# One pipeline over batches for the last two stages of a two-layer gated cross-attention kernel

## Chip, core and metric

The kernel runs on one core of one Trainium2 chip. The metric is the device time of one execution in microseconds; the kernel before has a median of 1914.06 us over three runs (1909.35 to 1925.1).

## What is computed

Eight batches of 512 tokens of width 512 (fp32), with a context of 77 rows a batch. Four residual blocks follow one another:

```python
x = x + tanh(g_xattn[0]) * L0_xattn(layernorm(x), ctx, ctx, Wq, bq, Wk, bk, Wv, bv, Wo, bo)   # 16 heads
x = x + tanh(g_ffn[0])   * L0_ffn(layernorm(x), router, 8 routed experts (top 2), 2 shared)
# the last two are what the change touches
def L1_xattn(h, v):
    probs = softmax(einsum('bsd,bvd->bsv', h, v), axis=-1)
    return einsum('bsv,bvd->bsd', probs, v)
x = x + tanh(g_xattn[1]) * L1_xattn(layernorm(x), ctx)
def L1_ffn(x):                                  # D = 512, hidden = 2048
    h = act_quant(x) @ weight_quant(w1).T       # 8 bit per token, ternary weights
    h = silu(depthwise_conv3(h) + conv_b)       # three taps along the tokens
    return act_quant(h) @ weight_quant(w2).T
x = x + tanh(g_ffn[1]) * L1_ffn(layernorm(x))
```

## The kernel before

The program runs in four blocks, each with its own instruction stream for every engine and semaphores between them; a block ends with a barrier. `attention` and `experts` come first. They leave, in DRAM, the residual x2 and the results of the experts for each slot (`ys_d`), and the quantised weights `w1q_d` and `w2q_d`. A "row tile" is 128 tokens; a batch has four (TB = 4).

`fuse` (from L1360) is a software pipeline over batches. In step s it combines batch s + 1 (`combine_first`, `combine_second`, L1606 and L1613 on VectorE: x2 + gate1 * y1 + gate2 * y2, with y1 and y2 gathered by eight indirect DMAs from Pool, L1517), takes its statistics (`bn_stats`, L1589) and normalises it on ScalarE (L1580). In the same step batch s is transposed (L1684), scored against the context (L1691), exponentiated (L1568), transposed again (L1695, copied to `prT` in L1571) and multiplied with the context (L1701), and VectorE adds the residual (L1661) and takes statistics (L1666). Batch s - 1 is normalised (L1563), its row maxima are taken (L1633), it is rounded on ScalarE (L1576, copies that add and later subtract a large constant) and dequantised on VectorE (L1601). The residual x3 and the quantised xd are written to DRAM scratch (L1494, L1499). The inverse roots (`rstd`, L1523 and L1525) are on Pool.

`ffn` (from L1706) is a second pipeline over batches with f_ps as a ring of three PSUM banks (RING = 3) and three hidden buffers `h` (HB = 3). In round s TensorE first multiplies two of the four row tiles of batch s - 2 with w2 (`down(0)`, `down(1)`, 17 matmuls each, L1963 and L1965), transposes the maxima of batch s - 1 (`max_transposes`, L1998), and then runs the 16 up tiles of batch s (`up(m)`, eight matmuls each, L1988), with the row of scales (L2004) behind up 1 and the other two down tiles behind up 5 and up 11. At the end it transposes batch s + 1 (L2033), whose high and low parts ScalarE (L1871) and VectorE (`low`, L1917) write. For each up tile ScalarE writes the middle tap (L1854), VectorE adds the other two (`taps`, L1890 and L1893), and ScalarE applies silu (L1836). VectorE takes the absolute maxima over eight tiles at a time (`half_max`, L1901). The tiles of batch s - 1 are multiplied with the row of scales on Pool (L1826) and rounded by a ScalarE copy (`lift_tile`, L1841), in the places that `lifts` names. VectorE adds the result to x3 (`outputs`, L1883).

Every engine executes its instructions in the order written, so an instruction that waits holds up all behind it on its engine.

## Time and profile before

| | |
|---|---|
| median of three runs | 1914.06 us |
| the profiled execution | 1918.68 us, of which the span is 1917.2 us |
| TensorE busy in the span | 1653.6 us (86%), weight loads 1304.5 us |
| VectorE, ScalarE, Pool busy | 1137.7, 794.9 and 588.0 us |
| mean granted clock of TensorE | 0.904 of full speed |

Times of rows are microseconds from the start of the span. PE is TensorE (PEld its weight loads), DVE VectorE, ACT ScalarE, POOL Pool (GpSimd), SP the queue of SyncE; a q behind an engine's name is a DMA that its queue issues. Granted clock 1.0 is 2.4 GHz and 0.5 is 1.2 GHz. The busy time of matmuls overlaps from one to the next, so the pace of a run of matmuls is read from the timeline and not from the mean of one.

### The profile page before, as it was taken

To read this page: it belongs to the slowest core of one execution; us is meant where nothing else is said; L and a number is where in the kernel's file an instruction comes from. 1 tells how busy PE (TensorE), PEld (TensorE's weight loads), DVE (VectorE), ACT (ScalarE), POOL (GpSimd) and SP (SyncE) were. 2 spreads that over 40 slices of the span, in tenths; PEclk is the share of its full clock that TensorE was granted. 3 is DMA by queue.
4 is the path that set the end of the run, shared out by engine and by line. 5 is a ranking of instruction groups with operands and counts; after the bars stand their busy time and mean duration, and the time that the engine had idled before them with its cause. 6 is when DMAs were issued, how large, how long until landed. Compare 5 with 4: busy or idle time off the path is not lost. (4 is left out here: it accounts for less than half of the span.)

```text
span 1917.2 us, 26044 instructions
## 1 busy us (share of the span) xinstructions
PE 1653.6 (86%) x8636; PEld 1304.5 (68%) x8636; DVE 1137.7 (59%) x1946; ACT 794.9 (41%) x1417; POOL 588.0 (31%) x541
## 2 busy tenths in 40 slices
PE   7599999999866999998999999837674889999997
PEld 5578888788745888886778888624343666666664
DVE  3587878878745344532223333258875777777775
ACT  2243433434313422222334443325563556566653
POOL 0133323333212444464331000065513243344440
PEclk9798989889967999999999999957666899999999
DMA  3112122121129889984443333287743111111102
GB/s 124 44 45 88 55 77 88 44 88 55 67 74 351 286 304 316 321 282 138 162 139 107 107 108 106 94 303 287 256 148 110 44 44 66 66 66 38 51 23 88
DMA packets 108196, 252.02 MB, mean 131 GB/s; under 512 B 15027, under 2 KB 15027, under 8 KB 103912
## 3 DMA queue, kind: packets, MB, share of 16 engines
q1 hardware_dynamic: 65272, 121.98, 19.0%
q0 software_dynamic: 17056, 67.12, 9.7%
q10 hardware_dynamic: 25808, 62.14, 9.2%
q8 instruction: 35, 0.57, 0.1%
q14 instruction: 25, 0.20, 0.0%
HBM read 147.13 MB, written 101.97 MB: 130 GB/s over the span
## 5 line engine op out<-in xcount | busy, mean ns | idle before, releaser
L1275 PE MATMUL e_u_ps<-e_w,e_xeT 128*128 128x512 f32 x1596 | 393.1, 398 | 10.8 <-DVE e_xeT L1180 10.8
L1275 PEld LDWEIGHTS e_u_ps<-e_w,e_xeT 128*128 128x128 f32 x1596 | 293.1, 189 | 73.3 <-DVE e_w L1229 8.9
L1988 PE MATMUL b_f_ps<-b_xdT,w1q 128*128 128x512 f32 x1024 | 254.1, 404 | 11.5 <-DVE b_h L1893 9.4
L1988 PEld LDWEIGHTS b_f_ps<-b_xdT,w1q 128*128 128x128 f32 x1024 | 191.4, 190 | 64.8 <-DVE b_h L1893 18.3
L1826 POOL TENSOR_TENSOR b_h<-b_h,b_srow 128x512 f32<-128x512 f32 x112 | 143.6, 1342 | 245.9 <-ACT b_srow L1847 245.9
L1286 PE MATMUL e_y_ps<-e_w,e_hT 128*128 128x512 f32 x798 | 209.9, 405 | 4.3 <-DVE e_hT L1211 2.8
L1286 PEld LDWEIGHTS e_y_ps<-e_w,e_hT 128*128 128x128 f32 x798 | 143.3, 190 | 31.0 <-issue 4.0
L1854 ACT ACTIVATE b_h<-b_f_ps,cb,cw 128x512 f32<-128x512 f32 x128 | 104.2, 814 | 124.5 <-PE b_f_ps L1988 124.3
L1890 DVE SCALAR_TENSOR_TENSOR b_h<-b_f_ps,cw,b_h 128x511 f32<-128x511 f32 x128 | 95.9, 749 | 85.9 <-ACT b_h L1854 85.7
L490 ACT ACTIVATE pT<-t_ps 77x512 f32<-77x512 f32 x128 | 71.9, 590 | 119.0 <-PE t_ps L691 119.0
L465 POOL TENSOR_TENSOR prob<-prob,ri 128x1232 f32<-128x1232 f32 x32 | 74.9, 2341 | 115.3 <-DVE ri L572 115.3
L1211 DVE TENSOR_TENSOR e_hT<-e_h_ps,e_hT 128x256 fp32r<-128x256 f32 x69 | 29.3, 424 | 134.8 <-ACT e_hT L1046 134.8
L1965 PE MATMUL b_o_ps<-w2q,b_h 128*128 128x512 bf16 x448 | 106.2, 392 | 0.0
L730 PE MATMUL m_ps<-wo,oT 128*128 128x512 f32 x384 | 96.3, 407 | 7.1 <-DVE oT L598 7.0
L744 PE MATMUL m_ps<-xT,wq 128*128 128x256 f32 x768 | 98.3, 289 | 1.4 <-DVE xT L554 1.4
L1836 ACT ACTIVATE b_h<-b_h 128x512 f32<-128x512 f32 x128 | 86.7, 677 | 30.8 <-DVE b_h L1893 30.8
L1893 DVE SCALAR_TENSOR_TENSOR b_h<-b_f_ps,cw,b_h 128x511 f32<-128x511 f32 x128 | 96.2, 752 | 4.5
L691 PE MATMUL t_ps<-ident,prob 128*77 128x128 f32 x512 | 90.8, 340 | 7.6 <-ACT pT L490 4.9
L744 PEld LDWEIGHTS m_ps<-xT,wq 128*128 128x128 f32 x768 | 95.4, 196 | 1.8 <-DVE xT L554 1.8
L442 POOL TENSOR_TENSOR ve<-mv,eps 128x2 f32<-128x2 f32 x32 | 6.2, 194 | 289.6 <-DVE mv L583 289.6
L730 PEld LDWEIGHTS m_ps<-wo,oT 128*128 128x128 f32 x384 | 73.0, 194 | 27.9 <-DVE oT L598 11.5
L985 POOL DMA_INDIRECT slots_in_scratch<-e_srow,e_scol x64 | 71.8, 1122 | 56.7 <-DMA e_srow<-xn_scratch 37.3
(221 smaller groups left out, 2869.1 us busy)
## 6 DMA issues: line engine op xcount, KB each, us to landing
e_xe<-slots_in_scratch SPq DMA_DIRECT2D x69, 256.0 KB, 2.6
experts_out_scratch<-e_ye ACTq DMA_DIRECT2D x69, 256.0 KB, 2.0
xin<-in_x SPq DMA_DIRECT2D x16, 512.0 KB, 3.8
xres<-in_x SPq DMA_DIRECT2D x16, 512.0 KB, 4.5
x_scratch<-x SPq DMA_DIRECT2D x32, 256.0 KB, 2.1
xn_scratch<-xn SPq DMA_DIRECT2D x32, 256.0 KB, 2.1
e_xe<-xn_scratch SPq DMA_DIRECT2D x32, 256.0 KB, 4.2
e_fraw<-in_w1T ACTq DMA_DIRECT2D x8, 1024.0 KB, 8.3
```

The source lines that it names most:

```text
L691: mm = pe.transpose(t_ps[0:C, t[("p", j, g)] % 2, i * P:(i + 1) * P], prob[:, j, g * HG + i, :], ident[:])
L730: mm = pe.matmul(m_ps[:, m[f"w{j}"] % 2], oT[:, pa, k, j * P:(j + 1) * P], wo[:, pb, k, :], start=(k == 0 and (pa, pb) == PASSES[0]), stop ...
L744: mm = pe.matmul(m_ps[:, m[f"q{i}"] % 2, g * W2:(g + 1) * W2], wq[:, pa, k, mt * P:(mt + 1) * P], xT[:, pb, k, :], start=(k == 0 and (pa, ...
L1275: mm = pe.matmul(u_ps[:, i], xeT[:, pa, k], w[:, par, pb, k * 2 * HID:(k + 1) * 2 * HID], start=(k == 0 and (pa, pb) == PASSES[0]), stop=( ...
L1286: mm = pe.matmul(y_ps[:], hT[:, pa, i * KH + k], w[:, par, pb, W1N + k * D:W1N + (k + 1) * D], start=(i == 0 and k == 0 and (pa, pb) == PA ...
L1826: pool.tensor_tensor(ht, ht, srow[:], ALU.mult).then_inc(u_done, 1)
L1836: act.activation(ht, ht, ACT.Silu).then_inc(h_done, 1)
L1854: act.activation(tile(s, m), f_ps[:, (s * KF + m) % RING], ACT.Identity, bias=cb[:, m:m + 1], scale=cw[:, m, 1:2]).then_inc(mid_tap, 1)
L1890: dve.scalar_tensor_tensor(out=ht[:, 1:S], in0=f[:, 0:S - 1], scalar=cw[:, m, 0:1], in1=ht[:, 1:S], op0=ALU.mult, op1=ALU.add).then_inc(pr ...
L1893: dve.scalar_tensor_tensor(out=ht[:, 0:S - 1], in0=f[:, 1:S], scalar=cw[:, m, 2:3], in1=ht[:, 0:S - 1], op0=ALU.mult, op1=ALU.add).then_in ...
L1965: mm = pe.matmul(o_ps[:, j % 2], rounded(s - 2, k, j), w2q[:, k, :], start=False, stop=(k == KF - 1))
L1988: mm = pe.matmul(f_ps[:, u % RING], w1q[:, k, m * P:(m + 1) * P], xdT[:, part, k], start=(k == 0 and part == 0), stop=(k == KD - 1 and par ...
```

## The change

`fuse` and `ffn` are replaced by one block, `tail`. A round s (from -2 to 9) holds what is still to be done for five batches:

- `down`: the four down tiles of batch s - 2 and its output (D0 to D3 below). All four stand ahead of the up tiles of the round now. The two `attend` banks and the down tiles share the two banks of o_ps.
- `quant`: maxima, scales, products and lifts of batch s - 1. Ten of the 16 products on Pool stand ahead of the combining, six behind it.
- `up`: the 16 up tiles of batch s with their taps and silus. The ring has four banks (RING = 4), which the transposes of the fusing part use too. There are two hidden buffers (HB = 2) in place of three.
- `cross`: the whole fusing part of batch s + 1, spread over the instruction streams between the up tiles. The quantised batch is not sent to DRAM any more but transposed in the same round.
- `comb_next`: the combining of batch s + 2. ScalarE multiplies y1 and y2 with their gates (`gate_experts`), Pool makes the two additions into the residual X, which stays on chip until the output (four buffers, XB = 4), and Pool issues the gathers two row tiles ahead, right behind the additions that free a buffer.

The dequantisation and the small steps of the inverse root move from VectorE to Pool. The order in which each engine takes the parts of a round is written out in the `run` of each engine.

```diff
         experts(nc, n)
-
-        n.w1q = keep("w1q", [P, KD, DH], FR)
-        n.w2q = keep("w2q", [P, KF, D], BF16)
-        n.cw = keep("cw", [P, KF, 3], F32)
-        n.cb = keep("cb", [P, KF], F32)
-        n.g2 = keep("g2", [P, 1], F32)
-        fuse(nc, n)
-        ffn(nc, n)
+        tail(nc, n)
...
+    RING = 4
+    HB = 2
+    XB = 4
...
+        X = sb("x", [P, XB, TB, D])
+        y = sb("y", [P, 4, D])
...
+            for s in range(-2, B + 2):
+                run(s, 0 <= s - 2, 0 <= s - 1 < B, 0 <= s < B, 0 <= s + 1 < B, s + 2 < B)
...
+        lifts = {0: (3,), 1: (4,), 2: (5,), 3: (6,), 4: (7,), 5: (8,), 6: (9,), 12: (10,), 13: (11,), 14: (12,), 15: (13, 14, 15)}
...
         @block.sync
+            def run(s, down, quant, up, cross, comb_next):
+                if down:
+                    sp.wait_ge(y_done, (s - 1) * TB)
+                    sp.dma_start(n.tile_rows(n.out, (s - 2) * TB, TB), X[:, (s - 2) % XB]).then_inc(out_done, 16)
+                if comb_next:
+                    if s + 2 >= XB:
+                        sp.wait_ge(out_done, (s - 1) * 16)
+                    load(s + 2)
...
         @block.gpsimd
+            def combine(b, j):
+
+                t = b * TB + j
+                xb = X[:, b % XB, j]
+                pool.wait_ge(gated, t + 1)
+                pool.wait_ge(x2_in[b % XB], 16 * (b // XB + 1))
+                pool.tensor_tensor(xb, xb, y[:, 2 * (j % 2)], ALU.add).then_inc(comb_first, 1)
+                pool.wait_ge(comb_first, t + 1)
+                pool.tensor_tensor(xb, xb, y[:, 2 * (j % 2) + 1], ALU.add).then_inc(comb, 1)
+                if t + 2 < B * TB:
+                    hold(pool, comb, t + 1, n.passed_pool)
+                    gather((t + 2) // TB, (t + 2) % TB)
...
+                if s == 0:
+                    column_sums()
+                if quant and up:
+                    pool.wait_ge(row_done, s)
+                    products(0, 10)
+                if comb_next:
+                    combine(s + 2, 0)
+                    combine(s + 2, 1)
+                if cross:
+                    rstd(1, mv2_done, s + 1, nmr2_done)
+                if comb_next:
+                    combine(s + 2, 2)
+                    combine(s + 2, 3)
+                if cross:
+                    for j in range(TB):
+                        pool.wait_ge(q_done, (s + 1) * TB + j + 1)
+                        pool.tensor_scalar(xw[:, j], xw[:, j], MAGIC, dq[:, j:j + 1], ALU.subtract,
+                                           ALU.mult).then_inc(xd_done, 1)
+                if quant and up:
+                    products(10, KF)
+                if comb_next:
+                    rstd(0, mv1_done, s + 2, nmr1_done)
...
         @block.scalar
+                def gate_experts(j):
+                    t = (s + 2) * TB + j
+                    act.wait_ge(y_in[j % 2], 32 * (t // 2 + 1))
+                    for i in range(2):
+                        yb = y[:, 2 * (j % 2) + i]
+                        ins = act.activation(yb, yb, ACT.Copy, scale=gate[:, i, t:t + 1])
+                    ins.then_inc(gated, 1)
+
+                b = s + 1
+                if cross:
+                    act.wait_ge(nmr1_done, b + 1)
+                    if b >= 1:
+                        act.wait_ge(xdt_full, b * TB)
+                    for j in range(TB):
+                        act.activation(xw[:, j], X[:, b % XB, j], ACT.Identity, bias=nmr[:, 0, j:j + 1],
+                                       scale=rs[:, 0, j:j + 1]).then_inc(xn_done, 1)
+                    for j in range(TB):
+                        act.wait_ge(xt_full, b * TB + j + 1)
+                        act.activation(xT[:, j], f_tiles("x", b, j), ACT.Copy).then_inc(xt_copied, 1)
+                if quant:
+                    scale_row()
+                    if up:
+                        for m in range(3):
+                            lift_tile(m)
+                if cross:
+                    act.wait_ge(nm_done, b + 1)
+                    for j in range(TB):
+                        act.activation(pr[:, j], q_ps[:, 1, j, 0:C], ACT.Exp, bias=nm[:, j:j + 1],
+                                       accum_out=su[:, j:j + 1]).then_inc(e_done, 1)
+                if up and s >= 2:
+                    act.wait_ge(y_full, (s - 1) * TB)
+                if up and s == 0:
+                    act.wait_ge(cw_done, 2)
+                if up and s == 1:
+                    act.wait_ge(wsum_steps, 4)
+                for m in range(KF):
+                    if up:
                         act.wait_ge(f_full, s * KF + m + 1)
+                        act.activation(tile(s, m), f_bank("f", s, m), ACT.Identity, bias=cb[:, m:m + 1],
                                        scale=cw[:, m, 1:2]).then_inc(mid_tap, 1)
                         if m >= 1:
                             silu(m - 1)
+                    if cross and m == 1:
+                        act.wait_ge(p_full, b + 1)
+                        act.activation(prT[:], q_ps[0:C, 0], ACT.Copy).then_inc(p_copied, 1)
+                    if quant and up:
+                        for r in lifts.get(m, ()):
+                            lift_tile(r)
+                    if comb_next and m in (2, 3, 5, 6):
+                        gate_experts(m - 2 if m < 4 else m - 3)
+                    if cross and m == 7:
+                        act.wait_ge(nmr2_done, b + 1)
+                        for j in range(TB):
+                            act.activation(xw[:, j], X[:, b % XB, j], ACT.Identity, bias=nmr[:, 1, j:j + 1],
+                                           scale=rs[:, 1, j:j + 1]).then_inc(x4_done, 1)
+                    if cross and m == 10:
+                        act.wait_ge(sc_done, b + 1)
+                        for j in range(TB):
+                            act.activation(xw[:, j], xw[:, j], ACT.Copy, bias=MAGIC,
+                                           scale=sc[:, j:j + 1]).then_inc(q_done, 1)
+                if up:
                     silu(KF - 1)
                 elif quant:
                     for m in range(KF):
                         lift_tile(m)
+                if cross:
                     for j in range(TB):
+                        act.wait_ge(xdt_full, b * TB + j + 1)
+                        act.activation(xdT[:, 0, :, j], f_tiles("d", b, j), ACT.Copy).then_inc(xdt_hi, 1)
...
         @block.vector
+                if down:
                     outputs(0)
                     outputs(1)
                 if quant:
                     token_scales()
+                if down and (up or not quant):
+                    outputs(2)
+                    outputs(3)
+                if cross:
+                    dve.wait_ge(s_full, b + 1)
+                    dve.tensor_reduce(nm[:], q_ps[:, 1, :, 0:C], AX.X, ALU.max, negate=True).then_inc(nm_done, 1)
+                for m in range(KF):
+                    if up:
                         taps(m)
+                    if cross and m == 0:
+                        dve.wait_ge(e_done, b * TB + TB)
+                        dve.reciprocal(ri[:], su[:]).then_inc(ri_done, 1)
+                        dve.wait_ge(ri_done, b + 1)
+                        dve.tensor_scalar(rt[:], ri[:], tg[:, 1:2], None, ALU.mult).then_inc(rt_done, 1)
+                        dve.wait_ge(rt_done, b + 1)
+                    if cross and m in (2, 4):
+                        fused(m - 2)
+                        fused(m - 1)
+                    if cross and m == 4:
+                        aggregate(1, stats[0] - TB, mv2_done)
+                    if cross and m in (7, 8):
+                        row_max(2 * m - 14)
+                        row_max(2 * m - 13)
+                    if cross and m == 8:
+                        row_scales()
+                    if up and m == 10:
+                        half_max(0)
+                if quant and not up:
                     dve.wait_ge(row_done, s)
                     for m in range(KF):
                         ht = tile(s - 1, m)
                         dve.tensor_tensor(ht, ht, srow[:], ALU.mult).then_inc(u_done, 1)
                         if m in (3, 7):
                             outputs(2 + m // 4)
+                if comb_next:
+                    for j in range(TB):
+                        dve.wait_ge(comb, (s + 2) * TB + j + 1)
+                        dve.bn_stats(st[:, 0, j], X[:, (s + 2) % XB, j]).then_inc(st_done, 1)
+                    stats[0] += TB
+                    aggregate(0, stats[0] - TB, mv1_done)
+                if cross:
                     low(0)
+                if up:
                     half_max(1)
+                if cross:
                     for j in range(1, TB):
                         low(j)
...
         @block.tensor
+                if s == B + 1:
                     down_all()
                     return
+                if down:
+                    down_tile(0)
+                    down_tile(1)
+                if cross:
+                    normed_transposes()
                 if quant:
                     max_transposes()
+                if down:
+                    down_tile(2)
+                if quant:
                     scale_row()
+                if down:
+                    down_tile(3)
+                if cross:
+                    scores()
+                for m in range(KF):
+                    if up:
+                        up_tile(m)
+                    if cross and m == 0:
+                        prob_transposes()
+                    if cross and m in (1, 3):
+                        attend(m - 1)
+                        attend(m)
+                if cross:
+                    quantised_transposes()
```

In `normed_transposes` row tile j waits for its bank, last read by `low(j)` of the batch before; `attend(2)` and `attend(3)` wait for `fused(0)` and `fused(1)`; `down_tile(2)` waits for `outputs(0)`.

## Rows read from the trace of the kernel before

**Rows 1.** Stretches: length, then each engine's busy us, granted clock, DMA share, GB/s.

```profile
1315.42:1337.19 21.77, 14.75 (x62) 9.20 (x61) 18.65 (x46) 12.54 (x26) 10.74 (x14) 0.69 0.72 251
...
1671.00:1724.40 53.40, 49.88 (x222) 34.53 (x221) 38.65 (x46) 32.85 (x53) 20.53 (x16) 0.97 0.17 60
```

**Rows 2.** Timeline, stage boundaries: start, us, engine, line, instruction, idle before it.

```profile
1242.02 0.34 ACTq L1058 DMA_DIRECT2D experts_out_scratch<-e_ye  x1
...
1270.72 2.93 ACT L1580 ACTIVATE f_xn<-f_x,nmr,f_rs 128x512 f32<-128x512 f32 x4 [28.86 <-DVE nmr L1649]
...
1457.80 0.20 POOL L1812 MEMSET b_lift<- 128x128 bf16 x1 [12.38 <-POOLq L1364]
...
1469.80 10.54 PE L1988 MATMUL b_f_ps<-b_xdT,w1q 128*128 128x512 f32 x44 [1.41 <-DVE b_xdT L1917]
...
1895.24 0.53 PEld L1972 LDWEIGHTS b_f_ps<-b_wsum,b_lift 128*128 128x128 bf16 x3
```

**Rows 3.** Timeline of TensorE: down, up, scores, attended tiles, maxima transposes.

```profile
1608.12 3.62 PE L1965 MATMUL b_o_ps<-w2q,b_h 128*128 128x512 bf16 x16
...
1716.40 4.46 PE L1965 MATMUL b_o_ps<-w2q,b_h 128*128 128x512 bf16 x16
...
1620.66 7.71 PE L1988 MATMUL b_f_ps<-b_xdT,w1q 128*128 128x512 f32 x32
...
1315.42 3.69 PE L1691 MATMUL f_s_ps<-f_ctraw,f_xT 128*128 128x77 f32 x32
...
1371.53 7.20 PE L1701 MATMUL f_o_ps<-f_craw,prT 77*128 77x512 f32 x8 [0.68 <-ACT prT L1571]
...
1615.25 1.04 PE L1998 MATMUL b_q_ps<-ident,b_am 128*128 128x128 f32 x8
```

**Rows 4.** Groups by line, VectorE, both stages: count, busy us, mean ns, idle before.

```profile
L1893 DVE SCALAR_TENSOR_TENSOR b_h<-b_f_ps,cw,b_h 128x511 f32<-128x511 f32 x128 | 96.2, 752 | 4.5
...
L1901 DVE TENSOR_REDUCE b_am<-b_h 128x512 f32<-128x4096 f32 x16 | 70.6, 4410 | 0.7 <-ACT b_h L1836 0.7
...
L1666 DVE BATCH_NORM_STATS2 f_st<-x 128x6 f32<-128x512 f32 x32 | 22.0, 686 | 0.1
```

**Rows 5.** Timeline of ScalarE: tap, silu, two lifts, four normalisations.

```profile
1854.12 0.81 ACT L1854 ACTIVATE b_h<-b_f_ps,cb,cw 128x512 f32<-128x512 f32 x1
...
1854.82 0.66 ACT L1836 ACTIVATE b_h<-b_h 128x512 f32<-128x512 f32 x1
...
1855.39 1.22 ACT L1841 ACTIVATE b_h<-b_h 128x512 f32<-128x512 f32 x2
...
1307.20 2.92 ACT L1580 ACTIVATE f_xn<-f_x,nmr,f_rs 128x512 f32<-128x512 f32 x4
```

**Rows 6.** Timeline of ScalarE around the first silu of the stage.

```profile
1473.84 0.81 ACT L1854 ACTIVATE b_h<-b_f_ps,cb,cw 128x512 f32<-128x512 f32 x1 [1.06 <-PE b_f_ps L1988]
...
1474.67 1.28 ACT L1836 ACT_TABLE_LOAD   x1
...
1475.96 0.67 ACT L1836 ACTIVATE b_h<-b_h 128x512 f32<-128x512 f32 x1
```

**Rows 7.** Pool: groups by line (as rows 4), and from issue to landing of L1517.

```profile
L1826 POOL TENSOR_TENSOR b_h<-b_h,b_srow 128x512 f32<-128x512 f32 x112 | 143.6, 1342 | 245.9 <-ACT b_srow L1847 245.9
...
L1525 POOL TENSOR_TENSOR f_rs<-f_ve,f_half 128x4 f32<-128x4 f32 x16 | 16.4, 1026 | 1.3
...
L1546 POOL TENSOR_SCALAR cw<-cwr,mean 128x48 f32<-128x48 f32 x1 | 0.4, 437 | 0.0
...
L1517 POOL DMA_INDIRECT y<-experts_out_scratch,ycol x64 | 64.0, 999 | 23.7 <-issue 16.7 <-POOL ycol L1513 6.7 <-DVE f_mv L1595 0.3
...
DMA to landing us min/median/max: 3.4/6.3/8.9
```

**Rows 8.** DMA issues of the fusing stage: count, KB each, us to landing.

```profile
f_x<-x_scratch SPq DMA_DIRECT2D x8, 1024.0 KB, 10.5
...
cwr<-in_conv_w SPq DMA_DIRECT2D x1, 24.0 KB, 12.1
```

715 lines of the change are left out of this document (257 added, 458 removed).

## The prediction

> **What bounds the kernel now.** I read the table of stretches first, then the boundaries of the stages in order of time, then the rows of one round of each stage. Up to 1242 us attention and experts run; the diff leaves them alone. The fusing stage reaches from there to 1457.8, the feed-forward stage to the end at 1917.2 [rows 2]: 215.8 + 459.4 = 675.2 us that the change rewrites. A fusing round takes 21.8 us, of which VectorE is busy 18.7 and TensorE 14.8 at a granted clock of 0.69. A feed-forward round takes 53.4 us; TensorE is busy 49.9 of them at 0.97, VectorE 38.7, ScalarE 32.9, Pool 20.5 [rows 1]. The up tiles run at 1.93 (32 matmuls in 7.7) and a down tile takes 3.7 with the one matmul ahead of it [rows 3]. So the first is bound by VectorE, the second by TensorE, and one batch costs 75.2 us in both. The remaining 675.2 - 8 x 75.2 = 74 us are beginnings and ends.
>
> **What the merged round costs each engine.** The arithmetic work of a batch stays; what goes is the x3/xd round trip (hidden, but for the 12 us from 1457.8 to the first up tile at 1469.8 [rows 2]).
> - TensorE: 49.9, plus 16 transposes (about 2.2, twice the eight of 1.04), scores 3.7, four transposes of probabilities (0.6) and four attended tiles. Their eight instructions took 7.2 at the low clock (1.2 GHz), so 3.6 at 2.4. Sum 60 [rows 1, 3].
> - ScalarE: 32.9 + two normalisations of 2.9 + four rounding copies 2.5 + xT copies 2.4 + exps 1.3 (four of 77 columns, estimated at half a full copy each) + prT 0.6 + eight gatings 5 (a 128x512 ACTIVATE issues every 0.6 to 0.7) + two table loads 2.6 = 53 [rows 1, 5, 6]. Exp and Silu need different tables and now alternate; before, each was loaded once in these stages.
> - VectorE: 38.7 + fused additions and both statistics (4 x 0.75 + 8 x 0.69) + row maxima (2.7, at 0.69) + small ones 2 = 52 [rows 1, 4]. The combining additions and the dequantisation leave it.
> - Pool: 20.5 + eight additions at 1.3 (row: 1.34) + eight gathers at 1.3 + four dequantisations 5 + two rstd (one power at 1.03 and three small steps each, 4) = 50 [rows 1, 7]. The dequantisation (128x512 TENSOR_SCALAR) has no row on Pool; between 0.44 (the 48-column one) and 2.1 (its slope from 0.2 extended) I take 1.3, like the two-input row. It lies between the q copies and the last six products, whose lifts ScalarE reaches later: 0 us at 1.3, 2 us at 2.1 (the next down tile waits for the last lift).
>
> **Where the round's time comes from.** No engine is full at 60, so order decides. I walk one full round; 0 is the end of TensorE's last quantised transpose. All costs are from [rows 3 to 7].
> - Front (TensorE). D0, D1 (3.67 each) end at 7.3. VectorE meanwhile does four statistics, low 0, half_max 1 (4.4), low 1 to 3, and is through at 9.1. The transposes of normalised rows need low j's PSUM bank, so they end at 9.8. Maxima 10.8, D2 14.5, scale row 15.5, D3 19.2, scores 22.9. No down tile overlaps the up tiles any more: with HB = 2 ScalarE may not write tile 0 before D3 is read out, where before two down tiles lay between up tiles. The row with the first down tile of a round at 4.46 instead of 3.62 [rows 3] shows 0.8 us for a clock that fell in the sparse tail of the round; I put the front at 23.3.
> - Head of the up tiles. Up 0 and the transposed probabilities (after max and exps) and up 1 end at 27.8. prT, without which attend 0 can't start, stands on ScalarE behind middle tap 1 (0.8), the Silu table (1.3) and silu 0 (0.6): copied at 31.1. TensorE waits 3.3 us there with up 2 behind attend 0 and 1. Up 2 ends 34.9, its tap 35.7, gate 0 ends 38.0.
> - Gather chain. Pool can't combine row tile 0 before 38.0. Two additions 2.7, 0.8 from a held wait to a gather (6.7 us over eight batches, in the row of the gathers), the second gather at 42.8 (1.0 + 0.3 later), tile 1 the same: its second gather starts at 48.5. A gather lands 3.4 to 8.9 us after issue, median 6.3 in a stage whose DMA share was 0.72. Here that share is about 0.2, so I take 4 (near the minimum): landed 52.5. ScalarE reaches gate 3 at about 50.5 and waits 2; gate 3 ends 53.7. All middle taps queue behind it.
> - Residual. Batch s+2's load waits on the SP queue for the store of batch s-2, which starts when D3 is read out (20). At 10.5 us for either 1 MB transfer [rows 8] it is in by 41, and Pool wants it at 38: 3 us at most. That row is from the stage with a DMA share of 0.72, so I take 0.
> - Tail. Tap 7, silu 6, four normalisations: 57.9. Tap 8, its VectorE taps 60.2, row maxima and scales 62.1, taps 9 63.6, silu 9, q copies 66.7. VectorE: taps 10, half_max 0 to 69.4, taps 11 70.9. Then four tiles with one lift each (0.70 + 0.57 + 0.62 = 1.9 on ScalarE): last middle tap 76.5, taps 78.0, last quantised transpose and last lift 78.7.
> Round: 79 us, 55.7 of them from up 0 to the last transpose, against 75.2 before. The merged engines' idle time is in-order waiting.
>
> **The table loads, by row and by page.** The row shows the load beginning 0.02 us after the ACTIVATE before it and Silu beginning 0.01 after it [rows 6]: 1.28 us in all. The Trainium skill (ScalarE: Activation LUTs, What ACT_TABLE_LOAD costs) adds a drain of about 1380 ns to every switch. By that the load on prT's path would cost 1.4 us more, some 10 us over seven rounds, and the forecast would be about 1952. The rows show no such gap, so the sum goes without it.
>
> **Sum.**
> - Start, 1242.4 to up 0 of batch 0: Pool waits for the constants before its first addition. They landed 12.1 us after issue behind two 1 MB loads and the gathers, at about 1260 [rows 8]; one 1 MB load less is ahead of them now, so I take 1257.8 (bounds 1252 to 1262). Four combining steps alternate with gathers (two of them issued only after tile 0 and 1): Pool is through at about 1280.7, rstd 1.9, normalisation at 1282.7, where before it was at 1270.7 [rows 2]. Scores, exps and attended tiles at the low clock, fused 1304; two more gather landings before x4, dequantised 1327, batch 1's transposes and scores before up 0: 1337.5. So 95 us (bounds 87 to 103).
> - Round 0, no lifts and no down tiles: 54 + front of round 1 (no D) 18 = 72.
> - Rounds 1 to 5: 5 x 79 = 395.
> - Round 6, without gates: 51 + front of round 7 (no scores) 17 = 68.
> - Round 7 (TensorE's 16 up tiles, 33.5), D0, D1, maxima, D2, scale row, D3 17, then from the last batch's down tiles to the end as before, 1895.2 to 1917.2 = 22 [rows 2]: 72.5.
> Together 702.5 against 675.2: +27.3. On the profiled span 1917.2 this is a span of 1944.5; with the 1.5 us around it, 1946. The median of the runs lies 4.6 below the profiled run's 1918.7, so I forecast 1942 us, 1.5% slower.
>
> **Rivals.**
> - *Latencies are absorbed and the round becomes engine-bound (faster).* If the prT copy and gate 3 find their inputs ready (a gather landing within 2 us, no waiting at attend 0), the up part falls from 55.7 to what VectorE needs: 16 x 1.45 + 6 + 3.2 + 4.4 + 2 = 39, plus 3 before its first tap and 3 for the last: 45. Six rounds of 11 less: 1876 us. For it: ScalarE, VectorE and Pool all have over 25 us idle per round in my walk, so there is idle time to recover. Against: prT stands in one queue behind a table load and a tap whose input comes after it. It decides below 74.8 us a round (4.2 less). Chance 0.22.
> - *No measurable change.* The start is 8 shorter and each round 2 to 3 shorter (a gate nearly in time, up tiles' taps closer together): 1916 us. Chance 0.17.
> - *The low clock settles in (slower still).* From up 11 on TensorE works less than half the time, as in the fusing round, whose granted clock was 0.69 [rows 1]. If D0 to D2 run at the low level (7.3 each instead of 3.7, the first two half hidden), the front grows by 5: six rounds, +30: 1972 us. Against: 0.97 in the feed-forward rounds, which have the same sparse transposes. Chance 0.14.
> - *A gather lands in 6.3 as before:* +2.3 a round, 1958; within the forecast's own range.
> Forecast 0.47, own range 1925 to 1965 (start +-8, landing 3.4 to 6.3, dequantisation 0 to 2 and residual 0 to 3 us a round).
>
> About 1% is what a measurement of this kernel can tell from no change. Faster by over 1% (below 1895): the first rival and a little of the second, 0.24. Within 1%: the second and the low end of the forecast, 0.20. Slower: 0.56. The range 1885 to 1975 leaves out most of the first rival, 0.16, and a few hundredths above.
>
> **What would show it.** Right: about 79 us between the maxima transposes of successive rounds; TensorE waiting 3 us at attend 0 for prT; ScalarE waiting for y (gather) before gate 3 and Pool for gate 0; 15 or so table loads of 1.28; up 0 of batch 0 near 1337; an end near 1944. Wrong: TensorE over 85% busy in a round; no wait at the gates; a round below 75; rows of the gated tiles or Pool's dequantisation far from 0.6 and 1.3; D tiles at 7 us.

## The result and the profile after

The changed kernel takes **2008.5 us** (median of four runs, 2001.4 to 2010.0), the kernel before 1914.1 in the runs beside it (median of three; a fourth took 4084.6 us and is left out). The ratio of the means is **1.047 (1.041 to 1.054)**, slower by 4.7%. The forecast was slower by 1.5% (1942 us), its range ended at 1975.

The page of the changed kernel, its span and the busy times of the engines:

```profile
span 2007.7 us, 25829 instructions
...
PE 1673.9 (83%) x8636; PEld 1319.0 (66%) x8636; DVE 1081.7 (54%) x1826; ACT 850.1 (42%) x1493; POOL 737.0 (37%) x660
```

The table of stretches (the columns of [rows 1]): one full round, then within it up tile 1 with the wait behind it, the 10 us that follow, and a stretch near the round's end.

```profile
1587.20:1672.50 85.30, 68.33 (x289) 46.60 (x288) 51.44 (x78) 52.87 (x88) 49.82 (x44) 0.86 0.17 54
...
1601.30:1606.70 5.40, 2.08 (x11) 1.40 (x9) 3.55 (x6) 4.26 (x7) 3.83 (x4) 0.96 0.73 253
1606.70:1616.70 10.00, 8.70 (x20) 5.32 (x20) 2.16 (x3) 3.58 (x7) 0.00 (x0) 0.68 0.00 0
...
1646.70:1665.00 18.30, 11.91 (x44) 7.05 (x43) 14.11 (x21) 11.84 (x21) 14.19 (x13) 0.70 0.00 0
```

One merged round takes 85.3 us where the two rounds of [rows 1] took 75.2. ScalarE, VectorE and Pool are busy 53, 51 and 50 us of it, as the sums in the prediction had it (53, 52, 50). TensorE is busy 68, not 60: the granted clock is 0.86 over the round and 0.68 in the 10 us behind the wait of 1603 to 1607.

The timeline at the boundaries that answer [rows 2]: last store of the experts, the constants' wait, the first up tile of batch 0, a first down tile:

```profile
1244.27 0.34 ACTq L1047 DMA_DIRECT2D experts_out_scratch<-e_ye  x1
...
1267.80 0.41 POOL L1628 TENSOR_SCALAR t_cw<-t_cwr,mean 128x48 f32<-128x48 f32 x1 [14.90 <-DMA t_cb<-in_conv_b]
...
1349.99 2.09 PE L1898 MATMUL t_f_ps<-t_xdT,t_w1q 128*128 128x512 f32 x8
...
1575.59 5.31 PE L1876 MATMUL t_o_ps<-t_w2q,t_h 128*128 128x512 bf16 x16
```

TensorE at the head of the up tiles (up 1; attended tiles 0 and 1; up 2 and 3):

```profile
1601.30 2.08 PE L1898 MATMUL t_f_ps<-t_xdT,t_w1q 128*128 128x512 f32 x8
1606.73 3.78 PE L1948 MATMUL t_o_ps<-t_craw,t_prT 77*128 77x512 f32 x4 [3.35 <-ACT t_prT L1695]
1609.52 5.91 PE L1898 MATMUL t_f_ps<-t_xdT,t_w1q 128*128 128x512 f32 x16
```

ScalarE in the same round: table load, silu 0, the copy of the probabilities; middle tap 2; gate 3; lift 10:

```profile
1604.24 1.28 ACT L1638 ACT_TABLE_LOAD   x1
1605.54 0.66 ACT L1638 ACTIVATE t_h<-t_h 128x512 f32<-128x512 f32 x1
1606.09 0.58 ACT L1695 ACTIVATE t_prT<-t_q_ps 77x512 f32<-77x512 f32 x1
...
1613.65 0.80 ACT L1689 ACTIVATE t_h<-t_f_ps,t_cb,t_cw 128x512 f32<-128x512 f32 x1 [6.42 <-PE t_f_ps L1898]
...
1631.31 1.34 ACT L1656 ACTIVATE t_y<-t_y,gate 128x512 f32<-128x512 f32 x2 [1.94 <-DMA t_y<-experts_out_scratch,slot]
...
1652.92 0.67 ACT L1643 ACTIVATE t_h<-t_h 128x512 f32<-128x512 f32 x1 [2.78 <-POOL t_h L1596]
```

Pool in the same round, the first addition, the dequantisations and the six late products:

```profile
1616.85 1.28 POOL L1561 TENSOR_TENSOR t_x<-t_x,t_y 128x512 f32<-128x512 f32 x1 [11.72 <-ACT t_y L1656]
...
1643.65 7.98 POOL L1614 TENSOR_SCALAR t_xw<-t_xw,t_dq 128x512 f32<-128x512 f32 x4 [1.76 <-ACT t_xw L1709]
1651.61 7.59 POOL L1596 TENSOR_TENSOR t_h<-t_h,t_srow 128x512 f32<-128x512 f32 x6
```

The groups by line (count, busy us, mean ns, idle before) of the operations that the sum priced: products, dequantisation, gates.

```profile
L1596 POOL TENSOR_TENSOR t_h<-t_h,t_srow 128x512 f32<-128x512 f32 x112 | 142.1, 1306 | 96.7 <-ACT t_srow L1649 96.7
...
L1614 POOL TENSOR_SCALAR t_xw<-t_xw,t_dq 128x512 f32<-128x512 f32 x32 | 63.8, 2000 | 28.0 <-ACT t_xw L1709 28.0
...
L1656 ACT ACTIVATE t_y<-t_y,gate 128x512 f32<-128x512 f32 x56 | 37.1, 712 | 27.3 <-DMA t_y<-experts_out_scratch,slot 27.3
```

The walk of a round, predicted and measured (us from the start of the round's first down tile, here 1575.2; the last transpose of the round before ended 0.2 us later):

| mark | predicted | after |
|---|---|---|
| up 0 starts | 23.3 | 23.6 |
| up 1 ends | 27.8 | 28.2 |
| probabilities copied | 31.1 | 31.5 |
| middle tap 2 starts | 34.9 | **38.5** |
| gate 0 ends | 38.0 | 41.6 |
| gate 3 ends | 53.7 | 57.5 |
| four normalisations end | 57.9 | 61.5 |
| q copies end | 66.7 | 70.2 |
| taps 11 end | 70.9 | 74.2 |
| round ends | 78.7 | **85.5** |

Two places carry nearly the whole difference of a round: 3.2 us between the copied probabilities and middle tap 2, and 3.5 us behind taps 11. Ahead of them and between them the walk holds within 0.4 us.

### The profile page after: what moved, and what is told of

It is laid out like the page before. It is cut to its first block and busy times, and to the rows that moved or that the text cites. A ratio compares the mean times of both kernels' runs of the same rounds, so it can differ in the third digit from the quotient of the medians.

```text
span 2007.7 us, 25829 instructions
## 1 busy us (share of the span) xinstructions
PE 1673.9 (83%) x8636; PEld 1319.0 (66%) x8636; DVE 1081.7 (54%) x1826; ACT 850.1 (42%) x1493; POOL 737.0 (37%) x660
## 3 DMA queue, kind: packets, MB, share of 16 engines
q1 hardware_dynamic: 48520, 90.53, 13.5%
## 5 line engine op out<-in xcount | busy, mean ns | idle before, releaser
L1898 PE MATMUL t_f_ps<-t_xdT,t_w1q 128*128 128x512 f32 x1024 | 278.1, 429 | 52.0 <-DVE t_h L1763 52.0
L1898 PEld LDWEIGHTS t_f_ps<-t_xdT,t_w1q 128*128 128x128 f32 x1024 | 204.5, 204 | 118.5 <-DVE t_h L1763 65.7
L1760 DVE SCALAR_TENSOR_TENSOR t_h<-t_f_ps,t_cw,t_h 128x511 f32<-128x511 f32 x128 | 95.4, 745 | 152.8 <-ACT t_h L1689 152.6
L1596 POOL TENSOR_TENSOR t_h<-t_h,t_srow 128x512 f32<-128x512 f32 x112 | 142.1, 1306 | 96.7 <-ACT t_srow L1649 96.7
L1689 ACT ACTIVATE t_h<-t_f_ps,t_cb,t_cw 128x512 f32<-128x512 f32 x128 | 103.3, 807 | 70.9 <-PE t_f_ps L1898 70.3
L479 ACT ACTIVATE pT<-t_ps 77x512 f32<-77x512 f32 x128 | 72.2, 591 | 120.6 <-PE t_ps L680 120.6
L1876 PE MATMUL t_o_ps<-t_w2q,t_h 128*128 128x512 bf16 x448 | 113.3, 411 | 0.0
L1638 ACT ACTIVATE t_h<-t_h 128x512 f32<-128x512 f32 x128 | 86.0, 672 | 43.1 <-DVE t_h L1763 42.8
L1643 ACT ACTIVATE t_h<-t_h 128x512 f32<-128x512 f32 x128 | 83.8, 678 | 36.4 <-POOL t_h L1596 34.5
L1763 DVE SCALAR_TENSOR_TENSOR t_h<-t_f_ps,t_cw,t_h 128x511 f32<-128x511 f32 x128 | 96.2, 752 | 4.5
```

Of the source, the lines that this page charges most:

```text
L1596: pool.tensor_tensor(ht, ht, srow[:], ALU.mult).then_inc(u_done, 1)
L1638: act.activation(ht, ht, ACT.Silu).then_inc(h_done, 1)
L1689: act.activation(tile(s, m), f_bank("f", s, m), ACT.Identity, bias=cb[:, m:m + 1], scale=cw[:, m, 1:2]).then_inc(mid_tap, 1)
L1760: dve.scalar_tensor_tensor(out=ht[:, 1:S], in0=f[:, 0:S - 1], scalar=cw[:, m, 0:1], in1=ht[:, 1:S], op0=ALU.mult, op1=ALU.add).then_inc(pr ...
L1763: dve.scalar_tensor_tensor(out=ht[:, 0:S - 1], in0=f[:, 1:S], scalar=cw[:, m, 2:3], in1=ht[:, 0:S - 1], op0=ALU.mult, op1=ALU.add).then_in ...
L1876: mm = pe.matmul(acc, rounded(s - 2, k, j), w2q[:, k, :], start=False, stop=(k == KF - 1))
```

## The experiments

Each kernel was timed on the same chip as the kernel before. The ratio to it stands first; the changed kernel's is 1.047. A round is the distance of two successive reductions of the transposed maxima on VectorE (L1745). Rounds 1 to 5 are the steady ones: in the changed kernel the first of them takes 83.1 us and the other four 85.2 to 85.3. The stages ahead, which are the same in every one of these kernels, ended anywhere between 1228 and 1245 us in the profiled executions, so the length of a round says more than the total of one execution. Diffs are extracts; "..." stands for lines left out.

**1. The copy of the probabilities ahead of middle tap 1.**

```diff
-                    if cross and m == 1:
+                    if cross and m == 0:
                         act.wait_ge(p_full, b + 1)
                         act.activation(prT[:], q_ps[0:C, 0], ACT.Copy).then_inc(p_copied, 1)
```

> Starts from the changed kernel (2008.5 us). ScalarE copies the transposed probabilities (prT) behind middle tap 0 instead of behind middle tap 1 and silu 0. Nothing is left out. Theory A (the wait of TensorE for this copy, 3.35 us a round, also drops TensorE's clock to its low level for the next tiles, which costs as much again): the wait goes, granted clock in the stretch behind it stays near 1.0, a round falls by 6 to 7 us (85.2 to about 79), 7 rounds give about 45 us: 1964. Theory B (only the wait counts, the tiles behind it are slow for another reason): 3.3 us a round, about 23 us: 1985. Theory C (the gathers and gates behind it set the round, the wait is covered): under 1 us a round, 2002 to 2008.

Ratio 1.021 (1.017 to 1.025), median 1958.9; a round takes 78.3. TensorE in its timeline (up 1, attended 0 and 1, up 2 and 3):

```profile
1558.30 2.09 PE L1898 MATMUL t_f_ps<-t_xdT,t_w1q 128*128 128x512 f32 x8
1560.22 1.88 PE L1948 MATMUL t_o_ps<-t_craw,t_prT 77*128 77x512 f32 x4
1561.54 4.21 PE L1898 MATMUL t_f_ps<-t_xdT,t_w1q 128*128 128x512 f32 x16
```

The wait is gone, the attended tiles take 1.88 instead of 3.78, the two up tiles 4.21 instead of 5.91. A round is 6.9 us shorter, twice the wait: theory A.

**2. TensorE kept busy through the wait.**

```diff
+                    if up and cross and m == 1:
+                        empty(f_uses, f_at, ("f", s, 2))
+                        for k in range(14):
+                            pe.matmul(f_bank("f", s, 2), w1q[:, k % KD, 0:P], xdT[:, 0, k % KD], start=True, stop=True)
                     if cross and m in (1, 3):
```

> Starts from the changed kernel. Its order and its waits are kept, but TensorE computes 14 matmuls of 128x512 whose result nobody reads into the free bank of up tile 2, between up tile 1 and the wait for the copied probabilities, about 3.3 us of work in the place of 3.35 us of waiting. Theory A (idling drops the clock): the attended tiles start within 0.5 us of where they did, but they and up tiles 2 and 3 take 1.8 and 1.93 us instead of 2.8 and 3, a round falls by about 3 us, total 1985 to 1990. Theory B (those tiles are slow for another reason, such as their operands or Pool's and VectorE's traffic): no change of the round, 2005 to 2012.

Ratio 1.033 (1.029 to 1.038), median 1982.4; a round takes 81.7. Its timeline (the matmuls that nobody reads, attended tiles, up 2 and 3):

```profile
1582.15 3.33 PE L1984 MATMUL t_f_ps<-t_xdT,t_w1q 128*128 128x512 f32 x14
1585.67 1.98 PE L1948 MATMUL t_o_ps<-t_craw,t_prT 77*128 77x512 f32 x4 [0.19 <-ACT t_prT L1695]
1587.09 4.21 PE L1898 MATMUL t_f_ps<-t_xdT,t_w1q 128*128 128x512 f32 x16
```

The attended tiles start no earlier relative to up 1 (3.4 us behind its end in either), and yet a round is 3.5 us shorter: theory A. Of the 6.9 us, half is the wait and half the low clock that follows it. This separates the two, which experiment 1 could not.

**3. Dequantisation back on VectorE**, behind taps 12 to 15, one tile each.

```diff
-                if cross:
-                    for j in range(TB):
-                        pool.wait_ge(q_done, (s + 1) * TB + j + 1)
-                        pool.tensor_scalar(xw[:, j], xw[:, j], MAGIC, dq[:, j:j + 1], ALU.subtract,
-                                           ALU.mult).then_inc(xd_done, 1)
...
+                    if cross and m >= 12:
+                        j = m - 12
+                        dve.wait_ge(q_done, b * TB + j + 1)
+                        dve.tensor_scalar(xw[:, j], xw[:, j], MAGIC, dq[:, j:j + 1], ALU.subtract,
+                                          ALU.mult).then_inc(xd_done, 1)
```

> Starts from the changed kernel. Only the four dequantisations of a batch go back from Pool to VectorE, one behind each of the taps 12 to 15. Nothing is left out. Theory A (Pool's 4 x 2.0 us delay products 10 to 15, ScalarE waits 2.8 us for product 10 ahead of middle tap 13, and that is on the path): lift 10's wait goes, a round falls by 2 to 3 us (85.2 to about 82.5), in all about 20 us with 8 us of it at the start where the batch 0 dequantisation is on the path too: 1985 to 1990. Theory B (the last stretch is bound by VectorE's taps, which now carry 2 us more): a round stays at 85 or rises by 1, total 2000 to 2012.

Ratio 1.033 (1.027 to 1.039), median 1986.6; rounds 2 to 4 take 81.7 us, round 5 85.2, at a lower granted clock (0.88 over that round; 0.90 to 0.92 in rounds 2 to 4). Lift 10 runs right behind the silu ahead of it (first fence, ScalarE's timeline), and the operation costs VectorE 0.48 us (second, groups by line):

```profile
1637.15 0.69 ACT L1633 ACTIVATE t_h<-t_h 128x512 f32<-128x512 f32 x1 [2.07 <-DVE t_h L1758]
1637.73 0.68 ACT L1638 ACTIVATE t_h<-t_h 128x512 f32<-128x512 f32 x1
```

```profile
L1833 DVE TENSOR_SCALAR t_xw<-t_xw,t_dq 128x512 f32<-128x512 f32 x32 | 15.4, 481 | 1.1 <-ACT t_xw L1704 0.8
```

Theory A, and with 3.5 us a round more than its 2 to 3. The same instruction takes 2.00 us on Pool and 0.48 on VectorE. Batch 0's alone, with nothing beside it, shortens the way from its score maxima to batch 1's from 47.7 to 42.0 us.

**4. The exponentials replaced by a copy with bias**, so that no table is switched. This kernel leaves out the softmax.

```diff
-                        act.activation(pr[:, j], q_ps[:, 1, j, 0:C], ACT.Exp, bias=nm[:, j:j + 1],
+                        act.activation(pr[:, j], q_ps[:, 1, j, 0:C], ACT.Identity, bias=nm[:, j:j + 1],
```

> Starts from the changed kernel. The four exponentials of a batch are replaced by a copy with bias, which needs no table of its own, so that the softmax is not computed and ScalarE's 14 table switches are gone but for one. Theory A (by the rows, the switch back ahead of silu 0 costs 1.28 us on the path to the copied probabilities, the other is hidden in a wait): TensorE's wait falls from 3.35 to about 2.1 us; if the clock still falls behind it, a round falls by 1.3 us, in all about 9 us: 1999. Theory A2 (the same, but the shorter wait keeps the clock up): 1.3 + 3.5 us a round, 1975. Theory B (a switch also drains the engine, about 1.4 us more that the rows don't show): 2.7 us a round, 1990, and the wait falls to 0.7 us.

Ratio 1.033 (1.029 to 1.037), median 1985.3; a round takes 82.0. TensorE (attended tiles, up 2 and 3):

```profile
1596.59 3.01 PE L1948 MATMUL t_o_ps<-t_craw,t_prT 77*128 77x512 f32 x4 [1.92 <-ACT t_prT L1695]
1598.61 5.27 PE L1898 MATMUL t_f_ps<-t_xdT,t_w1q 128*128 128x512 f32 x16
```

TensorE's wait for the copy is 1.92 us instead of 3.35, the same in all seven rounds that have a silu ahead of the copy: 1.43 us less. Of these, 1.28 is the load; without it, silu 0 also starts 0.1 us before middle tap 1 ends (1595.42 and 1595.52), an overlap that is lost where the load lies between them. Under theory B it would have been 2.7. The round fell by 3.2, more than the wait, and that number alone would not have told A2 from B. The attended tiles and up tiles 2 and 3 took 3.01 and 5.27 us, between the values of the changed kernel and of experiment 1, so they ran at the low clock for a shorter time. The outcome lies between A and A2; the exact split of the 3.2 us was not measured.

**5. Gates of tiles 0 and 1 ahead of the exponentials.**

```diff
+                if comb_next and up:
+                    gate_experts(0)
+                    gate_experts(1)
                 if cross:
                     act.wait_ge(nm_done, b + 1)
-                    if comb_next and m in (2, 3, 5, 6):
+                    if comb_next and m in ((5, 6) if up else (2, 3, 5, 6)):
```

> Starts from the changed kernel. ScalarE gates the expert rows of tiles 0 and 1 behind lifts 0 to 2, ahead of the exponentials (their gathers landed a round before), instead of behind middle taps 2 and 3; nothing is left out. The additions on Pool, and so the next gathers, can start some 10 us earlier. Theory A (gather, gate, additions and the fused normalisation behind them lie on the path): gate 3's wait for its gather (1.9 us) goes and four gates (2.3 us) leave the stretch before the normalised rows, a round falls by 3 to 4 us (85.2 to about 81.5), in all 1980 to 1987. Theory B (middle tap 2 and the tiles behind it set the pace because of the low clock): under 1 us a round, 2002 to 2010. The exponentials may start 0.7 us later in either.

Ratio 1.035 (1.031 to 1.039), median 1989.5; rounds 2 to 5 take 82.3 to 84.3. That is 2.4 us a round against the 3 to 4 of theory A: gates do lie on the path, but here they hold the exponentials up (they start 1.30 us behind the maxima of the scores instead of 0.04), and with them the probabilities.

**6. The constants' wait moved behind the first combining.**

```diff
+                if s == -1:
+                    pool.wait_ge(cw_in, 32)
...
-            pool.wait_ge(cw_in, 32)
             whole(run)
```

The two small instructions behind the wait (`cw`, `g2`) move with it.

> Starts from the changed kernel. Pool's wait for the convolution's constants, with the two small instructions behind it, moves from ahead of the first combining (15 us of waiting at the head of its queue) to behind the combining of batch 0. Nothing is left out. Theory A (that wait delays the first combining and so the whole pipeline's start): the first up tile of batch 0 comes 8 to 10 us earlier, total 1998 to 2001. Theory B (the load of the first x tiles lands no earlier than the constants do, being on the same queue ahead of them or sharing its bandwidth): start moves by under 2 us, total 2006 to 2010.

Ratio 1.046 (1.041 to 1.050), median 2009.7. The first combining comes 10 us earlier (1258.6), batch 0's score maxima only 2 us (60.1 us behind VectorE's last instruction of the experts instead of 62.3), and the next stretches give that back. Theory B. The transfers of the changed kernel from 1244 to 1300 us suggest why, and experiment 7 tests it: the busy share of the DMA engines in 40 slices, then issues with KB and us to landing.

```profile
DMA  2237999999999999997999994760016401650000
...
t_w1q<-w1q_scratch POOLq DMA_DIRECT2D x1, 4096.0 KB, 19.3
t_x<-x_scratch SPq DMA_DIRECT2D x3, 1024.0 KB, 18.5
t_w2q<-w2q_scratch SPq DMA_DIRECT2D x1, 2048.0 KB, 21.6
...
t_cb<-in_conv_b SPq DMA_DIRECT2D x1, 8.0 KB, 18.4
```

For some 30 us the DMA engines are 70% busy or more, in most slices over 90%. Of the 13.5 MB moved in this window, 6 are weights that nobody needs before 1340.

**7. The weights loaded later:** experiment 6, with the up weights' load behind the combining of tiles 0 and 1 and the down weights' load behind batch 0's attention. Both loads are taken out where they stood.

```diff
                     combine(s + 2, 1)
+                if s == -2:
+                    pool.dma_start(w1q[:].rearrange("p k f -> p (k f)"), n.w1q_d[:, :]).then_inc(w1_in, 16)
...
+                if s == 0:
+                    sp.dma_start(w2q[:].rearrange("p k f -> p (k f)"), n.w2q_d[:, :]).then_inc(w2_in, 16)
```

> Starts from the changed kernel. Only the start is rearranged: the constants' wait of Pool behind the combining of batch 0, the 4 MB load of the up weights behind the combining of tiles 0 and 1, the 2 MB load of the down weights behind batch 0's attention. Nothing is left out. Theory A (the start is bound by the bandwidth of the transfers, which are 97 to 99% busy for 28 us, and the gathers wait behind the weights): the first combining and the gathers behind it land 4 us after issue instead of 8, batch 0's maxima of the scores come 10 to 15 us sooner, total 1995 to 2000. Theory B (the weights are needed as early as they are loaded, so the first up tile waits for them instead): under 3 us, 2005 to 2012.

Ratio 1.038 (1.033 to 1.042), median 1989.1. Batch 0's score maxima come 50.0 us behind VectorE's last instruction of the experts instead of 62.3, and the rest takes 705 us in both: theory A, 12 us, of which 2 are experiment 6's and 10 the traffic's. The median is 19 us lower; the other 7 are probably no gain of the edit, since the stages ahead ended 7 us earlier in this profile. Its transfers, same view:

```profile
t_w1q<-w1q_scratch POOLq DMA_DIRECT2D x1, 4096.0 KB, 13.0
t_x<-x_scratch SPq DMA_DIRECT2D x3, 1024.0 KB, 10.3
```

**8. Experiments 1, 3 and 5 together.**

> Starts from the changed kernel and makes three edits at once: the probabilities copied behind middle tap 0, dequantisation back on VectorE behind taps 12 to 15, gates of tiles 0 and 1 ahead of the exponentials. Nothing is left out. Theory A (the costs lie one behind another on the same path and add): a round falls by 6.9 + 3.5 + 3 us, 85.2 to 72, total about 1915, beside the kernel before within 1%. Theory B (they cover one another, ScalarE or VectorE sets the middle of the round once the clock is up): a round at 75 to 77, total 1935 to 1950, still slower than before.

Ratio 1.009 (1.006 to 1.011), median 1935.3. Four of the five steady rounds take 74.3 to 76.0, the fifth 81.1. The single gains add to 12.8, the three together give about 10 in the four: between the theories, nearer B. Its stretch of taps 7 to 14 (columns as above) shows what comes next:

```profile
1598.10:1618.10 20.00, 14.23 (x49) 10.15 (x48) 18.12 (x27) 15.63 (x25) 14.14 (x12) 0.83 0.19 52
```

VectorE is busy 18.1 of 20 us there.

**9. Four edits:** the three, with gates 0 and 1 in ScalarE's wait ahead of the scale row, and the start of experiment 7.

```diff
+                if comb_next and up:
+                    gate_experts(0)
+                    gate_experts(1)
                 if quant:
                     scale_row()
```

> Starts from the changed kernel and joins four edits: probabilities copied behind middle tap 0, dequantisation on VectorE behind taps 12 to 15, gates of tiles 0 and 1 in ScalarE's 4.7 us wait ahead of the scale row (not ahead of the exponentials, where they held them up by 1.3 us in the run of three edits), and the later loads at the start. Nothing is left out. Theory A (the edits add, since the start and the rounds follow one another): the three edits gave 1935; the start gives 12 us (first maxima of scores 50 us behind the last expert tile instead of 62), the exponentials 1.3 us in each of 6 rounds: about 1915, within 1% of before (1919). Theory B (in the rounds VectorE is the bound by now, so the earlier exponentials give nothing): 1923. A round is 74 under A, 75.3 under B.

Ratio 1.002 (1.000 to 1.004), median 1925.2, with four steady rounds of 72.2 to 75.1 and one of 78.2: nearer theory B. The start's 12 us arrived. The exponentials again start 0.04 us behind the maxima, but a round gained less than their 1.3 us (74.3 on average in the four, against 75.0 in the four of experiment 8).

**10. VectorE's maximum over tiles 0 to 7 cut in two**, tiles 0 to 3 behind tap 5, tiles 4 to 7 behind tap 10.

```diff
-                    if up and m == 10:
-                        half_max(0)
+                    if up and m == 5:
+                        quarter_max(0)
+                    if up and m == 10:
+                        quarter_max(1)
```

`quarter_max` is `half_max` over four tiles; one VectorE maximum, ahead of `half_max(1)`, joins the two parts.

> As the kernel of four edits, and VectorE's maximum over tiles 0 to 7, 4.4 us at tap 10, is cut in two: tiles 0 to 3 behind tap 5, where VectorE waits for ScalarE, tiles 4 to 7 behind tap 10, and the two joined at the end of the round behind the tiles' last low part. Nothing is left out. Theory A (taps 7 to 15 are bound by VectorE, 18.1 of 20 us busy there): 2.2 us of it leave that stretch, a round falls by 1.5 to 2 us, 10 us in all below the kernel of four edits. Theory B (the wait behind tap 5 is no slack, since what follows it waits for the same chain): no difference, within 3 us.

Ratio 0.999 (0.997 to 1.001), median 1919.0: 6 us less than experiment 9 on the same chip, where A expected 10 and B at most 3. The five steady rounds take 74.1 on average instead of 75.0. In its timeline the next wait stands out, TensorE at attended tile 2 and ScalarE at middle tap 4:

```profile
1641.21 1.10 PE L1969 MATMUL t_o_ps<-t_craw,t_prT 77*128 77x512 f32 x2 [1.41 <-DVE t_x L1790]
...
1646.99 0.80 ACT L1692 ACTIVATE t_h<-t_f_ps,t_cb,t_cw 128x512 f32<-128x512 f32 x1 [5.23 <-PE t_f_ps L1919]
```

**11. Attended tiles 2 and 3 behind up tile 4**, added to experiment 10.

```diff
-                    if cross and m in (1, 3):
-                        attend(m - 1)
-                        attend(m)
+                    if cross and m in (1, 4):
+                        attend(m // 2)
+                        attend(m // 2 + 1)
```

> As the kernel with the maximum cut in two, and TensorE computes the attended tiles 2 and 3 behind up tile 4 instead of ahead of it. Nothing is left out. There they wait for VectorE to free the two banks (1.4 and 0.3 us), and with them up tile 4, for which ScalarE then sat idle 5.2 us; the granted clock in those 10 us is 0.83. Theory A (that wait, and the low clock in it, are on the path): up tile 4 comes 3 to 4 us sooner, a round falls from 74.5 to 71 or 72, 15 to 20 us in all, about 1900: faster than before by 1%. Theory B (the fused rows, the normalisation behind them and VectorE's later taps are the path; up tile 4 early gives only an earlier wait): within 4 us of the kernel it starts from, 1915 to 1923.

Ratio **0.990 (0.986 to 0.993)**, median 1904.1; five steady rounds of 71.4 on average, 2.7 less. Theory A: the in-order queue of TensorE had kept up tile 4, which was ready, behind an attended tile that waited for its bank. ScalarE no longer waits ahead of middle tap 4. How much of the 2.7 us is the wait and how much the clock behind it was not separated. Behind the sparse end of a round the first down tile still runs at the low clock (TensorE: last quantised transposes, first down tile):

```profile
1598.41 1.11 PE L1976 MATMUL t_f_ps<-ident,t_xw 128*128 128x128 f32 x4 [0.94 <-DVE t_xw L1851]
...
1599.75 5.56 PE L1897 MATMUL t_o_ps<-t_w2q,t_h 128*128 128x512 bf16 x16
```

**12. Matmuls that nobody reads in those pauses**, added to experiment 11.

```diff
+                        empty(f_uses, f_at, ("d", b, j))
+                        for k in range(4 if up and j > 0 else 0):
+                            pe.matmul(f_bank("d", b, j), w1q[:, k, 0:P], w1q[:, k, 0:4 * P], start=True, stop=True)
                         pe.wait_ge(xd_done, b * TB + j + 1)
-                        empty(f_uses, f_at, ("d", b, j))
```

> As the kernel with the later attended tiles, and TensorE computes four matmuls of 128x512 that nobody reads ahead of each of the quantised transposes of tiles 1 to 3, where it waits 1.4, 1.2 and 0.7 us for VectorE. Theory A (the pauses of the last 10 us of a round let the clock fall, so that the first down tile behind them takes 5.4 us instead of 3.6): that tile takes 3.6 us, a round falls by 1.8 us, 10 us in all. Theory B (the down tile is covered, the path runs through VectorE's maximum behind it, or the filling delays the transposes as much as it saves): within 4 us of the kernel it starts from.

Ratio **0.988 (0.984 to 0.992)**, median 1899.0; the same five rounds take 70.5. The same stretch in experiment 11 and in this one, where it is one round; then the filling matmuls and the first down tile:

```profile
1526.00:1596.10 70.10, 63.48 (x286) 44.26 (x284) 52.55 (x83) 51.60 (x87) 41.87 (x40) 0.91 0.21 65
...
1526.00:1596.10 70.10, 62.47 (x302) 44.20 (x301) 53.93 (x85) 53.13 (x89) 41.95 (x40) 1.00 0.22 65
...
1655.04 1.22 PE L1975 MATMUL t_f_ps<-t_w1q 128*128 128x512 f32 x4 [0.21 <-DVE t_h L1766]
...
1656.74 3.62 PE L1897 MATMUL t_o_ps<-t_w2q,t_h 128*128 128x512 bf16 x16
```

The clock is 1.00 over this round (0.93 to 1.00 in the five, 0.90 to 0.93 in experiment 11) and the first down tile takes 3.62 instead of 5.56. In the steady rounds this gave 0.9 us each on average, half of theory A's 1.8; where the other half went was not traced; the totals of 11 and 12 (1904 and 1899) differ by less than their runs spread, so in the total the gain is likely, not shown.

## Why the prediction was right in direction and short in size

**Right: the waits and the engine sums.** No engine is the bound, the waits of the in-order queues are. TensorE waits 3.35 us at attended tile 0 (said: 3.3), gate 3 waits 1.94 us for its gather (said: 2), which landed 3.8 us after issue (said: 4), Pool waits 11.7 us for gate 0, the front takes 23.6 (said: 23.3). A gate instruction takes 0.71 us as it lies between others. The residual's load cost nothing. The rivals with a faster or an equal time needed those waits to be absorbed, and none was.

**Wrong step 1, the clock behind the wait.** The walk priced the wait of 3.3 us for the copied probabilities and then ran attended tiles and up 2 at the high level (2.4 GHz). The row of the slow down tile, 4.46 instead of 3.62 [rows 3], had been read as 0.8 us for the sparse tail only, and the rival on the low clock looked at the down tiles alone. It compared the tail with the fusing round as one where TensorE "works less than half the time", but the row of that round has it busy 14.75 of 21.77 us [rows 1]. Behind the wait TensorE ran at a mean of 0.68 for 10 us, and middle tap 2 came 3.6 us later than walked. Experiments 1 and 2 show it: 6.9 us for wait and clock, 3.5 for the clock alone. Over rounds 1 to 5 that is 17 of the missing 31 us.

**Wrong step 2, the price of the dequantisation on Pool, and what queues behind it.** The bounds were 0.44 and 2.1 us; I took 1.3, like the two-input row, with 0 us on the path. It takes 2.00, near the upper bound as written, whose price of 2 us a round stood in the text; the row shows lift 10 waiting 2.8 us, and experiment 3 gives 3.5 for the whole. My 2 us assumed that only the last lift is late. But lift 10 stands ahead of middle tap 13 in ScalarE's queue, so the taps behind it are late with it. The upper bound was also worked out wrong: 0.2 us and the slope of the 48-column row (0.24 us for 48 columns) give 2.7 us for 512 (an estimate), not 2.1. So neither row had the price; the measured 2.00 lies halfway between 1.3 and 2.7. The fault is that a middle value with 0 us on the path was taken where the row left a range of 0.44 to 2.7. Five rounds: 14 to 17 us.

**Wrong step 3, the start.** Said 95 us from the last expert store to up 0, measured 105.4. The constants landed at 1267.8, not 1257.8, since I priced them with the row of the fusing stage [rows 8] and one load less ahead. The last of them, the 8 KB of the convolution's bias, took 18.4 us to land, as the rows of experiment 6 show; 6 MB of weights that this program loads in the same stretch were not in the sum. Even so the wait named in the sum was not the cost: without it (experiment 6) 2 us come back, without it and the traffic (experiment 7) 12. Batch 0's dequantisations, which nothing hides there, took 8.0 us where 5.2 were assumed.

**The sum.** Start 105.4 for 95, round 0 78.4 for 72, rounds 1 to 5 426.2 for 395, the rest 153.1 for 140.5: 763.1 for 702.5. The stages ahead ended 2.3 us later. Step 1 is in every round (experiment 2 takes 3.5 us out of round 0 too), step 2 in the start and in rounds 1 to 6 (out of round 0 experiment 3 takes 0.5), step 3 in the start. What is left over, some 2 us in round 0 and 6 us behind round 5, was not traced.

**The table switches.** The trace shows 14 loads of 1.28 us in these stages. The seven ahead of a silu begin right behind the ACTIVATE before them (0.1 us of idle time for all seven), and silu 0 follows 0.02 us behind its load, in the rows above. The Trainium skill's rule (ScalarE: Activation LUTs, What ACT_TABLE_LOAD costs) of a further drain of about 1380 ns would have put 2.7 us into the wait; experiment 4 took 1.43 out. For the switches of this kernel the rule does not hold, and the sum was right to go by the row.

**Where the gain of the merge was.** After the waits were taken out one by one, a steady round fell from 84.8 us to 70.5 on average of the five, below the 75.2 of the two separate rounds, and the merged kernel is faster than before by 1.2%. That lies between the forecast and the engine-bound rival (68 us a round, 1876 us), which even this version does not reach. Nor does it show that merging alone gives 1.2%: edits such as the maximum cut in two were not tried on the kernel before.

## What to carry to other kernels

Where two stages are merged into one in-order pipeline, a wait of TensorE costs itself and can cost what the clock loses behind it, as much again behind the 3.35 us here; walk the tiles behind such a wait at the low level as well, or give the engine something to compute. In a queue, look not at how long an operation takes but at what stands behind it: copies that another engine waits for belong ahead of taps whose own input is late, and attended tiles that wait for a bank behind tiles that don't. Where an operation has no row on its engine, carry both ends of the range of its price through the walk, with all that queues behind it, and count the transfers that share the stretch before calling one small load's wait the cost.

## What the runs showed of the hardware that was not expected

- A TENSOR_SCALAR of 128x512 with a per-row operand takes 2.00 us on Pool, longer than a TENSOR_TENSOR of that size (1.31), and 0.48 on VectorE.
- Small TENSOR_SCALARs of VectorE stretch in the merged pipeline. The 128x4 one that scales the reciprocal sums, first before, then after:

```profile
L1655 DVE TENSOR_SCALAR rt<-f_ri,tanh_gates 128x4 f32<-128x4 f32 x7 | 1.6, 230 | 0.3
```

```profile
L1821 DVE TENSOR_SCALAR t_rt<-t_ri,tanh_gates 128x4 f32<-128x4 f32 x8 | 4.5, 561 | 0.3
```

  Its shortest took 229 ns, its longest 1389; the reciprocal just ahead of it kept 168. The seven long ones fall while Pool computes (products, and in the longest case the column sums of the weights), but no run took that cause away, so this is an observation.
- A pause of 3.35 us at attended tile 0 was followed by some 10 us at a mean granted clock of 0.68; filled with matmuls that nobody reads (experiment 2), the 10 us from the attended tiles on had 0.96 and two up tiles took 4.21 us instead of 5.91.
